# An attention block on one core: stage one written out group by group, with its work moved between engines

## The reference

```
h = layernorm(x) * (1 + ca) + sa
q, k, v = split(h @ W_attn)             # 16 heads of 16 channels
att = softmax(causal(q k^T / 4)) * decay   # decay depends on the distance of query and key
x = x + ga * ((att @ v) @ W_proj)
h = layernorm(x) * (1 + cb) + sb
x = x + gb * (h @ (W + low-rank product)^T + b)
```

## Time and profile before

| what | value |
|---|---|
| median of 3 runs | 1375.11 us (1373.11 to 1375.23) |
| the profiled execution: its own time, its span | 1372.6 us, 1370.6 us |
| granted TensorE clock, mean | 0.991 of full speed |
| busy share of the span: PE, ACT, DVE, POOL | 91%, 93%, 71%, 14% |
| first DMA issue of the attention function | 134.28 us after the span's start |
| HBM traffic over the span | 41.74 MB read, 20.97 MB written |

### The profile page before, as it was taken

The page is one execution under the profiler, slowest core; times in us unless marked ns, Lnnn a source line. Parts: engine busy times, 40 slices in busy tenths (PEclk is TensorE's granted clock), DMA queues, the critical chain, the costliest instruction groups (busy, mean ns, idle before and its releaser), DMA issues.

```text
span 1370.6 us, 28808 instructions
## 1 busy us (share of the span) xinstructions
PE 1248.8 (91%) x11067; PEld 743.1 (54%) x11067; DVE 969.3 (71%) x2064; ACT 1278.3 (93%) x2643; POOL 189.6 (14%) x405
## 2 busy tenths in 40 slices
PE   7986999999999999999999999999999998888786
PEld 5553555555555555555555555555555554444443
DVE  3876677777777777777777777777777776655554
ACT  2555999999999999999999999999999999999995
POOL 0322000301102030302011030303020110303030
PEclk9998999999999999999999999999999999999999
DMA  4599511010100001010100000010101000000100
GB/s 153 192 322 277 165 56 28 21 28 20 28 20 10 24 16 29 20 28 21 28 21 24 16 15 24 20 28 21 28 17 28 17 20 17 12 25 17 28 1 18
DMA packets 94447, 64.62 MB, mean 47 GB/s; under 512 B 59595, under 2 KB 89570, under 8 KB 94306
## 3 DMA queue, kind: packets, MB, share of 16 engines
q1 hardware_dynamic: 94306, 62.75, 15.6%
HBM read 41.74 MB, written 20.97 MB: 46 GB/s over the span
## 4 chain that ended last, share of the span: by engine, by line
PE 37%; ACT 33%; DVE 7%; issue 7%; ACTq 0%; DVEq 0%
ACT fast_s_ps L1171 21%; PE fast_s_ps L927 17%; ACT fast_probs L1171 13%; PE fast_t_ps L984 7%; PE fast_t_ps L953 5%; PE fast_t_ps L969 5%; DVE fast_negmax L1248 3%; DVE fast_probsT L1267 2%; PE fast_t_ps L1015 2%; PE fast_s_ps L936 1%; PE fast_t_ps L995 1%; DVE fast_y_sb L1286 1%; DVE fast_probsT L1257 0%; PE fast_t_ps L1028 0%; PE fast_t_ps L1145 0%
## 5 line engine op out<-in xcount | busy, mean ns | idle before, releaser
L1171 ACT ACTIVATE fast_s_ps<-fast_s_ps,fast_negmax 128x1024 f32<-128x1024 f32 (+4 forms) x768 | 851.3, 1147 | 2.5 <-PE fast_s_ps L927 2.0
L927 PE MATMUL fast_s_ps<-k_stack,xq 96*128 96x512 bf16 (+3 forms) x2448 | 663.6, 354 | 68.3 <-ACT fast_probs L1171 36.8
L1171 ACT ACTIVATE fast_probs<-fast_s_ps,fast_negmax 128x640 f32<-128x640 f32 (+7 forms) x512 | 493.9, 965 | 5.8 <-DVE fast_negmax L1248 5.6
L1248 DVE TENSOR_REDUCE fast_negmax<-fast_s_ps 128x1 f32<-128x512 f32 (+3 forms) x512 | 339.6, 663 | 110.8 <-PE fast_s_ps L936 108.7
L1257 DVE TENSOR_TENSOR fast_probsT<-fast_t_ps,fast_dec_c 128x384 f32<-128x384 f32 (+2 forms) x512 | 276.3, 540 | 179.9 <-PE fast_t_ps L953 177.4
L927 PEld LDWEIGHTS fast_s_ps<-k_stack,xq 96*128 96x128 bf16 x2448 | 202.4, 98 | 327.4 <-ACT fast_probs L1171 106.7
L953 PE MATMUL fast_t_ps<-ident,fast_probs 128*128 128x128 f32 x1488 | 249.9, 275 | 15.5 <-DVE fast_y_sb L1286 15.5
L1171 ACT ACTIVATION_READ_ACCUMULATOR fast_s_ps<-fast_s_ps,fast_negmax 128x1 f32 x768 | 256.7, 334 | 0.0
L953 PEld LDWEIGHTS fast_t_ps<-ident,fast_probs 128*128 128x128 f32 x1488 | 182.9, 141 | 62.7 <-DVE fast_y_sb L1286 22.6
L1267 DVE TENSOR_TENSOR fast_probsT<-fast_t_ps,fast_dec_c 128x256 f32<-128x256 f32 x464 | 191.8, 413 | 11.6 <-PE fast_t_ps L969 0.5
L969 PE MATMUL fast_t_ps<-ident,fast_probs 128*128 128x128 f32 x912 | 187.3, 285 | 6.5 <-DVE fast_probsT L1267 0.4
(11 more groups left out here) (149 smaller groups left out, 701.1 us busy)
## 6 DMA issues: line engine op xcount, KB each, us to landing
parts_d<-part SPq DMA_DIRECT2D x24, 512.0 KB, 5.6
k_stack<-parts_d SPq DMA_DIRECT2D x96, 128.0 KB, 3.6
xq<-parts_d SPq DMA_DIRECT2D x384, 32.0 KB, 2.1
fast_vals<-v_d SPq DMA_DIRECT2D x36, 128.0 KB, 2.4
xq<-x_dram SPq DMA_DIRECT2D x8, 512.0 KB, 5.8
v_d<-wa_t SPq DMA_DIRECT2D x8, 512.0 KB, 5.6
xb<-x_dram SPq DMA_DIRECT2D x32, 128.0 KB, 2.1
out_dram<-xb SPq DMA_DIRECT2D x32, 128.0 KB, 1.8
```

The source lines that it names most:

```text
L927: return nc.tensor.matmul(s_ps[:, n % SLOTS, at:at + w], q, k_stack[:, h, k0:k0 + w], start=True, stop=stop)
L1171: nc.scalar.activation(dst, src, ACT.Exp, bias=negmax[:, p % 2, side, h:h + 1], scale=-1.0, accum_out=sums[:, p % 2, side, h, c:c + 1]).th ...
L1248: nc.vector.tensor_reduce(out=negmax[:, p % 2, side, h:h + 1], in_=s_ps[:, n % SLOTS, CW - P * min(MAXW, b1 - b0):CW], axis=AX_X, op=ALU.m ...
```

## The change

The loop of `paired` is gone: every engine's list is written out for g from 0 to 7. Besides, work is moved:

- VectorE normalises group g+2 and takes the statistics of g+3 while group g is in TensorE (before: g+1 and g+2). SP loads x for g+4 ahead of the stores of g (before: g+3).
- Both halves of `hT` are copied by ScalarE (`copy_hT`).
- The low part of groups 0 to 6 is made by VectorE (`lowest`), at the head of the next group's VectorE work. GpSimd works in the last group only.
- ScalarE makes the middle part of g-1 behind the first biased quarter of g (before: at the end of g's own work).
- VectorE adds the bias to v (`values_out`) ahead of the rest of the same group (before: behind it).
- In the last group ScalarE makes `middle(6)` behind a wait for the landing of the high store of group 6, and the four middle quarters come after all biased and high quarters.

SP's order of the stores, of `stack_keys` and of `load_queries` is the same. The core of the diff:

```diff
@@ sync
-                sp.wait_ge(xn_ready, 1)
-                load_x(2, 0)
...
-                    if g + 3 < NG:
-                        sp.wait_ge(xn_ready, g + 2)
-                        load_x(g + 3, 1 - b)
...
+                for g in range(2, 4):
+                    sp.wait_ge(xn_ready, g - 1)
+                    load_x(g, g % 2)
...
+                    if g + 4 < NG:
+                        sp.wait_ge(xn_ready, g + 3)
+                        load_x(g + 4, b)
@@ scalar
+                def copy_hT(g):
+
                     act.wait_ge(xnT_ready, g + 1)
-                    nc.scalar.copy(hT[b][:, 0, :], pt_ps[:, 0, :]).then_inc(hT_by_act, 1)
+                    if g >= 2:
+                        act.wait_ge(v_ready, g - 1)
+                    for cc in range(CH):
+                        last = nc.scalar.copy(hT[g % 2][:, cc, :], pt_ps[:, cc, :])
+                    last.then_inc(hT_by_act, 1)
...
+                def middle(g):
+
+                    act.wait_ge(rest1_ready, g + 1)
+                    if g >= 1:
+                        act.wait_ge(part_stored[1][(g - 1) % 2], ((g - 1) // 2 + 1) * 16)
+                    nc.scalar.copy(part[1][:], kq32[:, g % 2]).then_inc(mid_ready, 1)
...
+                for g in range(NG - 1):
+                    if g >= 2:
+                        act.wait_ge(low_ready, g - 1)
                     for m in range(4):
...
+                        biased_part(g, m)
+                        if m == 0 and g >= 1:
+                            middle(g - 1)
+                    copy_hT(g + 1)
+                    if g >= 1:
+                        act.wait_ge(part_stored[0][(g - 1) % 2], ((g - 1) // 2 + 1) * 16)
                     act.wait_ge(kq_out, g * 4 + 4)
...
+                    nc.scalar.copy(part[0][:], kq32[:, g % 2]).then_inc(high_ready, 1)
+                    if g + 3 < NG:
+                        std(g + 3, (g + 3) % 2)
+
+                g = NG - 1
+                act.wait_ge(a_step, 1)
+                nc.scalar.activation(tmp_c[:], cnd[:], ACT.Exp, scale=-1.0).then_inc(a_step, 1)
+                act.wait_ge(low_ready, g - 1)
+                biased_part(g, 0)
+                act.wait_ge(part_stored[0][(g - 1) % 2], ((g - 1) // 2 + 1) * 16)
+                middle(g - 1)
+                high_quarter(g, 0)
+                for m in range(1, 4):
+                    biased_part(g, m)
+                    high_quarter(g, m)
+                act.wait_ge(part_stored[1][(g - 1) % 2], ((g - 1) // 2 + 1) * 16)
+                act.wait_ge(low_ready, g)
+                for m in range(4):
+                    act.wait_ge(last_rest, m + 1)
+                    nc.scalar.copy(part[1][:, m, :], kq32[:, g % 2, m, :]).then_inc(last_mid, 1)
@@ gpsimd
-                    pool.wait_ge(mid_ready, g + 1)
-                    if first >= 1:
-                        pool.wait_ge(part_stored[2][1 - b], (k + b) * 16)
-                    nc.gpsimd.tensor_tensor(part[2][:], kq32[:, b], part[1][:], ALU.subtract).then_inc(low_ready, 1)
@@ vector
-                half_hT(0, 0)
...
+                def lowest(g):
+
+                    dve.wait_ge(mid_ready, g + 1)
+                    if g >= 1:
+                        dve.wait_ge(part_stored[2][(g - 1) % 2], ((g - 1) // 2 + 1) * 16)
+                    nc.vector.tensor_tensor(part[2][:], kq32[:, g % 2], part[1][:], ALU.subtract).then_inc(low_ready, 1)
...
+                dve.wait_ge(xnT_ready, 1)
+                normalise(1, 1)
+                measured(2)
+                for g in range(NG):
+                    if g >= 1:
+                        lowest(g - 1)
+                    if g + 2 < NG:
+                        dve.wait_ge(xnT_ready, g + 2)
+                        normalise(g + 2, g % 2)
+                    if g + 3 < NG:
+                        measured(g + 3)
+                    if g < NG - 1:
+                        values_out(g)
+                        dve.wait_ge(high_ready, g + 1)
+                        nc.vector.tensor_tensor(kq32[:, g % 2], kq32[:, g % 2], part[0][:], ALU.subtract).then_inc(rest1_ready, 1)
+                g = NG - 1
+                for m in range(4):
+                    dve.wait_ge(last_high, m + 1)
...
+                values_out(g)
```

187 lines of the change are left out of this document (57 added, 130 removed).

## The result

The changed kernel takes 1375.9 us in the median of 20 runs, the kernel before 1372.4 us beside it on the same chip: a ratio of 1.0021 [1.0012, 1.0030]. It is slower by 0.21%, that is 2.9 us (the medians over all runs lie 3.5 apart; the ratio goes by rounds). The profiled execution took 1375.4 us, its span is 1373.5 us. The three runs of before from which the prediction's level of 1375.1 us was taken lay 2.7 us above what the same kernel showed over 20.

What follows compares the result with a forecast made beforehand. Stage one was taken as bound by TensorE up to group 2, then transfers, with SP's list ending last. 4.9 - 0.9 - 0.4 = +3.6 us on 1375.1 gave 1378.7 us, 0.26% slower; range 1374.3 to 1381.3.

Steps and rivals of the forecast that it cites:

- T: Landing of group 6's high store: forecast 121.0 us instead of 122.76, after savings of 1.28 and 0.5.
- middle 1.90 and 0.08, low 2.29 and 0.04: Group 6 behind T: ScalarE's middle copy, VectorE's low part and hand-overs put low at 125.3 instead of 120.41.
- 4.9 - 0.9 - 0.4: End of stage one: later low part, less the last issues' wait and faster query loads; attention starts 3.6 us later.
- The last two issues don't wait: SP's last two store issues of group 7 find their quarters ready: 1.1 instead of 2.02 us, 0.9 back.
- The query loads, 0.4 back: SP's 12 query loads, 8.96 us before, get 0.4 us shorter with less traffic; range 0 to 1.8.
- 0.9 earlier: Low of group 1 lets SP's first key stacking start 0.9 us before 57.54; only 0.5 counted.
- 2.0 around it: Time of a profiled run outside its span, taken as 2.0 us: span 1374.2 makes 1376.2.
- VectorE isn't what ends the stage: GpSimd out of groups 0 to 5: normalising gets 3.76 us a group back, but the sum stays the same.
- the working for low of group 1: Sum from group 1's k and q work through transposes, v, bias, rest, middle and low: low comes at 56.6 us.
- Rival C: v bias before rest waits for the v store in groups 4 to 6: T 122.8, +5.4, 1380.5 us; chance 0.10.
- Loop written out, forecast 0 +- 0.4: Writing out the loop over groups 2 to 5 costs at most 0.1 us a group, 0.4 either side; taken as 0.
- The Trainium skill's fixed cost plus bytes: Fixed 2.0 us plus bytes at 436 GB/s: a 512 KB store lands in 3.2 us, T 117.9, sum +0.5 us.

Runs made afterwards that it cites:

- after, middle first, both queues: Changed kernel with middle(6) ahead of the wait for group 6's high store and six of 12 query loads issued by ScalarE: ratio 0.9965.

## Why the prediction was right and wrong

The marks of the kernels side by side (one profile each, us):

| kernel | ratio | G | G to S | S to T | T to A | A |
|---|---|---|---|---|---|---|
| before | 1 | 37.03 | 20.51 | 65.22 | 11.52 | 134.28 |
| after | 1.0021 | 36.28 | 19.55 | 63.98 | 15.90 | 135.71 |
| after, middle first | 1.0008 | 36.55 | 19.55 | 64.93 | 12.34 | 133.37 |
| after, rest first | 1.0014 | 34.00 | 18.45 | 63.93 | 15.89 | 132.27 |
| after, middle and rest first | 0.9989 | 34.07 | 18.45 | 63.44 | 12.34 | 128.30 |
| after, middle first, both queues | 0.9965 | 36.61 | 19.55 | 64.43 | 8.97 | 129.56 |
| the same and rest first | 0.9944 | 34.20 | 18.45 | 65.26 | 8.98 | 126.89 |
| before, with the wait | 1.0031 | 34.69 | 20.51 | 65.38 | 15.92 | 136.50 |
| before, written out | 1.0018 | 36.25 | 20.50 | 67.15 | 12.38 | 136.28 |
| before, GpSimd out | 0.9983 | 34.96 | 17.91 | 64.46 | 10.44 | 127.77 |
| that, with the wait | 1.0017 | 34.88 | 17.90 | 66.02 | 15.90 | 134.70 |

**The mechanism of the forecast** was right: the wait in front of `middle(6)` moves SP's list, and that list ends the stage. The step "middle 1.90 and 0.08, low 2.29 and 0.04" measured 4.23 us against 4.3. The size was too large: +3.6 us forecast for the start of attention, +1.43 measured in A and +2.18 from G to A.

**The step that failed is the sum behind T**, "4.9 - 0.9 - 0.4". It makes 16.9 us from T to A. Measured are 15.90, and 15.87 to 15.92 in all nine profiles that have the wait and leave the query loads where they are. Its terms went wrong both ways:

- "The last two issues don't wait", 0.9 us back: measured 2.02 us again. In the kernel after, VectorE's last low quarters are done at 130.09 and GpSimd's at 129.54, so nothing was left to wait for at 133.29. The two issues themselves take 0.79 and 1.13 us.
- The query loads, 0.4 back: measured 7.71 instead of 8.96, so 1.25 back.
- From the low part's end to the first query load, nothing back: measured 0.39 us instead of 1.34, so 0.95 back.

Together 2.2 us came back against the 1.3 forecast.

**T, forecast 121.0, measured 119.81.** Of the 1.2 us, 0.75 lie ahead of G, where the forecast had no term and where executions of kernels with the same list there differ by up to 3 us (33.88 to 36.92). From G to T it is 83.53 us, where the forecast makes 84.0; the eight profiles with the changed kernel's lists up to T have 83.4 to 84.5, so the rest of this step stands within their spread. Its first term, "0.9 earlier", measured 0.96, with some luck: it sets the low part's end against the issue of the stacking, which in before follows 0.48 us behind the low part (57.06, 57.54), and the low part came about 0.5 us sooner after G than summed. The reason for counting 0.5 of it isn't borne out in this pair, in which all of it reached T. The other term, 1.28 us for the x load that leaves the stretch, measured 1.24 here, 0.3 to 1.5 over the eight. From S on, the stage takes 63.4 to 67.2 us in every profile in which VectorE doesn't hold it up. Whether it is SP's issuing or the transfers that fix this length isn't settled: SP issues without a gap from 103.84 to 117.4, and issues take longer while the transfers are full (in the changed kernel 12 query loads take 9.0 us without the wait and 7.7 behind it). I had named the transfers alone.

**The time outside the span** was taken over from before, "2.0 around it". It is 3.8 us in the median of after. This is 1.7 of the 2.9 us measured, a term for which the forecast had nothing; without it the span grew by 1.5 us, less than half of the +3.6. That the time came out so near to the forecast is in part luck.

**GpSimd out** got no term at the end of the stage, since "VectorE isn't what ends the stage". By itself it is worth -0.17%. It moves the start of SP's list by 2.60 us, though VectorE doesn't end the stage. (In the working for low of group 1 the prediction has this gain, together with the wait for v; it didn't ask what each is worth.) Normalising did fall to 1.38 us everywhere. This is the Trainium skill's rule of the shared port pair (SBUF — State Buffer, "SBUF: two separate sides"), and the trace agrees: 1.38 us beside an idle GpSimd against 5.14 beside a busy one.

**Rival C's v bias in front of the rest** was given 0.10 and a price at the v store. No such price shows: from S to T the four kernels with the rest first take 63.4 to 65.3 us, the eight without it 63.8 to 64.9. The price is paid at group 1, where the rest waits for TensorE's v, and is 1.10 us between G and S, 0.11% by the ratio (0.19% by the pair with the middle first).

**Loop written out, forecast 0 +- 0.4**: on before it costs 0.18% (0.08 to 0.27), 2.5 us; on the kernel with GpSimd out it isn't settled. The bound was taken from TensorE's busy time alone, and no run shows in which list the cost arises.

**The Trainium skill's fixed cost plus bytes** (DMA: Bandwidth & Descriptors, "Anatomy of one DMA") gave 3.2 us, an estimate, for a 512 KB store. The section states this for DMAs that GpSimd issues; here SP issues them. The high store of group 6 landed 3.48 us after its issue at 116.33, so at this place the trace nearly agrees; before, it took 4.32. Where T was off by this rule (117.9) it was the issue, set at 114.7.

**The level.** Of the 1378.7 us forecast 2.7 were the three runs' excess over the kernel's own level of 1372.4. Measured against that level it is +2.9 us where +3.6 was forecast.

Put together from the ratios: GpSimd out -0.17%; tokens ahead, `hT` on ScalarE and written-out lists together +0.06% (0.9989 against 0.9983, no difference that can be told); the wait and the v bias before the rest +0.32% (1.0021 against 0.9989). The sum is the measured +0.21%. How the middle term divides stays open: the written-out lists may cost and the tokens ahead give back, and neither was undone by itself in the changed kernel.

## What to carry to other kernels

Find the queue whose list ends a stage and mark three points in it: where it fills, where the last outside event releases it, and where it ends. Count them from a point behind the start-up: here a fall of the clock in group 0 shifted all of them by up to 1.7 us from one execution to the next. An edit is worth what it moves at these points; a faster engine beside a full queue is worth the moment by which the queue starts earlier, and that isn't nothing. Before adding a wait on one engine, count what the other engines' lists have behind it: here a wait in a place where ScalarE had time to spare puts twelve DMA issues late. If an engine has a gap anyway, let it issue part of them on its own queue.
